# The inner groups of a three-stage layer kernel: a hardware loop or written out

## The reference

```python
x = x + xattn(layernorm(x), ctx, Wq, Wk, Wv, Wo, bo)   # 8 heads of 64, context 257 x 192 per sequence
x = x + attn(layernorm(x), ln_g, ln_b, Wx, Ww, bw, Wk, Wv, Wr, Wo)
#   w = sigmoid(xn @ Wx @ Ww + bw); k = xn @ Wk; v = xn @ Wv; r = sigmoid(xn @ Wr)
#   over the 32 rows: state = (1 - w) * state + k v^T;  out = r . state;  y = out @ Wo
x = x + ffn(layernorm(x), U1, V1, b1, U2, V2, b2)      # gelu(x @ U1 @ V1 + b1) @ U2 @ V2 + b2
```

## Time and profile before

| | |
|---|---|
| median of 3 runs | 1336.26 us (1333.10, 1336.26, 1339.06) |
| the profiled execution | 1338.63 us, span 1336.8 us |
| TensorE busy | 1109.4 us, 83% of the span |
| VectorE busy | 859.9 us, 64% |
| ScalarE busy | 788.3 us, 59% |
| GpSimd busy | 578.8 us, 43% |
| mean granted clock of TensorE | 0.973 |
| transfers | 73.88 MB, mean 55 GB/s |

### The profile page before, as it was taken

How to read it: one execution, slowest core, us unless ns; L and a number is a source line. 1 busy time by engine, 2 the same in 40 slices (tenths; PEclk the granted TensorE clock), 3 DMA queues, 4 the chain that set the end, 5 groups by cost and what they waited for, 6 DMA issues and landing times.

```text
span 1336.8 us, 26076 instructions
## 1 busy us (share of the span) xinstructions
PE 1109.4 (83%) x7880; PEld 906.3 (68%) x7880; DVE 859.9 (64%) x2340; ACT 788.3 (59%) x1886; POOL 578.8 (43%) x788
## 2 busy tenths in 40 slices
PE   3888888888888888888888888888888888888865
PEld 2767777685767758676676767667676776767643
DVE  3548477485856749477584857748485774848542
ACT  2656575665756556575665657566575756657521
POOL 1336245372534527254263625527362553725330
PEclk9899899999999999999999999999999999989976
DMA  6211112030221202122130211213021120302000
GB/s 231 75 47 57 50 51 71 22 99 14 63 64 43 75 22 69 44 63 58 33 91 22 63 50 55 64 35 91 22 63 50 49 69 22 102 11 63 21 8 8
DMA packets 49688, 73.88 MB, mean 55 GB/s; under 512 B 5697, under 2 KB 31425, under 8 KB 49665
## 3 DMA queue, kind: packets, MB, share of 16 engines
q1 hardware_dynamic: 42464, 65.06, 16.7%
q10 hardware_dynamic: 7200, 8.53, 1.9%
HBM read 68.98 MB, written 4.59 MB: 55 GB/s over the span
## 4 chain that ended last, share of the span: by engine, by line
PE 31%; issue 28%; DVE 23%; ACT 10%; POOL 6%; ACTq 1%; DVEq 1%; DMA 0%; POOLq 0%; SPq 0%
DVE probs L892 7%; PE gb L523 4%; PE gb L513 4%; PE gb L432 4%; ACT probs L690 3%; DVE xn L878 3%; PE scores L452 3%; PE gb L423 3%; PE ptp L470 2%; PE acc L491 2%; DVE ptl L905 2%; DVE tailp L900 2%; PE gb L415 2%; PE gb L579 2%; PE gb L588 1%
## 5 line engine op out<-in xcount | busy, mean ns | idle before, releaser
L1092 POOL TENSOR_TENSOR rstd<-ve,vecs 128x2 f32<-128x2 f32 x48 | 35.3, 736 | 395.8 <-DVE ve L869 395.8
L1075 POOL TENSOR_TENSOR t0l<-raw_t,t0h 128x258 fp32r<-128x258 f32 x128 | 95.2, 744 | 247.7 <-ACT t1s L679 247.7
L491 PE MATMUL acc<-pth,nat 128*128 128x256 f32 x768 | 172.8, 302 | 33.6 <-DVE ptl L905 33.2
L690 ACT ACTIVATE probs<-scores,nmax 128x257 f32<-128x257 f32 x256 | 119.1, 471 | 98.0 <-DVE nmax L885 97.8
L491 PEld LDWEIGHTS acc<-pth,nat 128*128 128x128 f32 x768 | 126.4, 188 | 48.4 <-DVE ptl L905 36.7
L470 PE MATMUL ptp<-ident_r,probs 128*128 128x128 f32 x512 | 84.3, 288 | 68.5 <-DVE probs L892 66.9
L491 PE MATMUL acc<-ptl,nat 128*128 128x256 f32 x512 | 137.4, 280 | 0.0
L979 DVE TENSOR_TENSOR qk_l<-gb,qk_h 128x512 fp32r<-128x512 f32 x128 | 83.8, 687 | 79.4 <-ACT qk_h L726 78.5
L702 ACT ACTIVATE pth<-ptp 128x512 fp32r<-128x512 f32 x128 | 76.6, 598 | 87.5 <-PE ptp L470 87.5
L706 ACT ACTIVATE pc<-acc 128x512 f32<-128x512 f32 x128 | 76.5, 598 | 81.2 <-PE acc L491 77.4
L892 DVE TENSOR_SCALAR probs<-probs,rinv 128x257 f32<-128x257 f32 x256 | 120.2, 511 | 4.5
(11 more groups left out here) (131 smaller groups left out, 3328.7 us busy)
## 6 DMA issues: line engine op xcount, KB each, us to landing
raw_t<-in_ctx_t SPq DMA_DIRECT2D x128, 258.0 KB, 2.8
raw_n<-in_ctx_n SPq DMA_DIRECT2D x128, 192.0 KB, 2.4
xin<-in_x SPq DMA_DIRECT2D x16, 256.0 KB, 2.9
out<-vt ACTq DMA_DIRECT2D x16, 256.0 KB, 3.5
tailc<-tail_scratch SPq DMA_DIRECT2D x64, 6.0 KB
wq<-in_wq SPq DMA_DIRECT2D x1, 512.0 KB, 3.7
wk_raw<-in_wk SPq DMA_DIRECT2D x1, 512.0 KB, 4.2
wo<-in_wo ACTq DMA_DIRECT2D x1, 512.0 KB, 5.2
```

What stands on the lines that cost most here:

```text
L491: last = mm(acc[:, i], w, x, start=k == 0, stop=k == len(terms) - 1)
L690: go(probs[:, r, 0:L], scores[:, r, 0:L], ACT.Exp, bias=nmax[:, r:r + 1], accum_out=rsum[:, r:r + 1]).then_inc(s["exp_ready"], 1)
L1075: p_.tensor_tensor(t0l[i][:], raw_t[i][:, 0], t0h[i][:].bitcast(F32), ALU.subtract)
```

## The change

`turns` calls the bodies for m = 0 to 13 with a number instead of opening a hardware loop, and so does SyncE. The order of instructions on each engine, their buffers and the values of all waits stay what they are; each wait is for a constant, each address is fixed. The program becomes longer: the loop's body stands in it fourteen times.

```diff
@@ turns @@
             body(Phase("a", 0))
             body(Phase("ab", 0))
-            with engine.Fori(0, NG - 2) as m:
+            for m in range(NG - 2):
                 body(Phase("abc", m))
             body(Phase("bc", 0))
             body(Phase("c", 0))
@@ block.sync, load_tails @@
-                    sp.dma_start(tailc[0:3, i:i + 2].bitcast(F32), scratch[:, bass.ds(g.index * G + 2 * pair, 2)])\
+                    sp.dma_start(tailc[0:3, i:i + 2].bitcast(F32), scratch[:, g.index * G + 2 * pair:g.index * G + 2 * pair + 2])\
                         .then_inc(tailc_in[pair % 2], 16)
@@ block.sync @@
             body(Phase("a", 0))
             body(Phase("ab", 0))
-            with sp.Fori(0, NG - 2) as m:
+            for m in range(NG - 2):
                 body(Phase("abc", m))
```

## The result

The changed kernel takes 1331.47 us (median of 16 runs, 1327.33 to 1333.82); the kernel before took 1334.55 beside it (16 runs, 1330.86 to 1339.06). The ratio is 0.9974, 95% interval 0.9962 to 0.9985: 3.1 us, a real gain, but a quarter of a per cent. Timed again later, the changed kernel gave 0.9969 (0.9958 to 0.9980). The result is inside the predicted range, on the forecast's side of no change, and less than half of the 8.4 us forecast; the prediction had called anything under 0.5% no more than "same".

What follows compares the result with a forecast made beforehand. No single engine bounded the kernel: TensorE held 31% of the chain of waits, VectorE 23%, "issue" 28%. Terms of 0.30 + 0.30 = 0.6 us a pass, times 14, took 8.4 from 1336.26, giving 1327.9 us; range 1315 to 1339.

Steps and rivals of the forecast that it cites:

- Registers, b = 2 to 7: Attention stretch between probability transposes of inner groups 2 and 7: register waits take 0.30 us a pass longer than constants.
- The twin: Written-out phase "ab", same work with constants: b = 2 to 7 takes 30.41 us against 30.71 in loop pass 2.
- hidden registers: Rival: the 0.30 us is another order of arrivals, handoffs are covered; time stays at 1336 (1331 to 1341); chance 0.20.
- more exposed: Rival: "issue" is partly registers in the uncompared 48 us; 1.3 us or more a pass, 1318 or less; chance 0.13.
- Handoffs elsewhere: Projections, b = 0 and 1, pass border: 0.14 us per handoff, two on the path, 0.30 us a pass (0 to 1.0).
- Branch and addresses: Engines' 14 jumps back and address arithmetic for 22 transfers a pass on SyncE and ScalarE: both worth 0.
- Code: Fetching written-out code all through the run costs 0.0 us; rival, packets waited for in full, 1374 us, chance 0.05.
- a gap that wanders: Sign of code cost: TensorE, VectorE or ScalarE gaps ending in "issue", moving through the pass with instruction packets.
- Clock: TensorE's clock falls at three of fifteen pass borders, one costing 2.84 us; a shorter period shifts them, direction unknown.
- the rival of 1362 us: TensorE's clock gives way at twelve more of fifteen pass borders, 2.84 us each, 34 us slower; clock rival's chance 0.10.
- The sum: Over 14 loop passes: 0.30 + 0.30 = 0.6 us a pass, 8.4 us less (ends 4 and 18), median 1327.9 us.

Runs made afterwards that it cites:

- late-wait kernel: Changed kernel with waits reordered so that the one ending last rides on the operation itself; 1330.97 us, ratio 0.9964 to the kernel before.

## Why the prediction was right, and where it was not

- **Registers, b = 2 to 7: the size right, the way only in part.** 0.30 forecast, 0.34 in this stretch, 0.29 over the pass; the kernel with VectorE alone written out has the 0.34. The prediction read the difference to "ab" as the price of register instructions in the path. At b = 3 to 4 these are at most 0.13 of the 0.55; 0.42 is the shorter pair at L892, and 0.3 is lost again behind it. The twin carried the same rearrangement, so the number came out; in that the rival "hidden registers", which spoke of another order of arrivals, was half right. Its forecast, a time unchanged, falls with the period, and so does "more exposed": the surplus of "issue" in the chain held no time that could be gained.
- **Handoffs elsewhere: the step that failed.** The term of 0.30 us a pass came from the one pair L979 and L432, which did gain (0.24 to 0.05). The step took it for the price of registers. It is the price of where the last wait stands, and writing out raises it at four other places by 0.10 each (L415 twice, L579, L985). The segment of a pass that holds the projections, between two of GpSimd's t0l steps, even takes 16.25 us instead of 16.06. The rest of the pass came out at 0.29 - 0.34 = -0.05, so the term was nothing, at its lower bound. That is also why the period, 78.29, reached neither the 77.9 to 78.1 that was to show the forecast right nor the 78.5 that was to show it wrong. 14 x 0.30 = 4.2 us of the 8.4 went there. Only a handoff that gains was read.
- **Branch and addresses: right**, worth 0; the period stayed at 78.55 with TensorE alone, and at 78.57 with ScalarE, GpSimd and SyncE.
- **Code: right.** 64 packets instead of 12 on the larger queue, four a pass where the prediction had three, and passes at full clock agree within 0.07 us, which leaves no room for a gap that wanders.
- **Clock: the open point was named, the form was not.** Falls did not spread to most borders, as the rival of 1362 us had it; the mean clock of the executions is that of before, 0.976. The changed kernel's falls cost 0.7 us each where before's cost 2.84. But the late-wait kernel shows the rival's mechanism at work: a pass 0.33 us shorter lost 0.54 us to falls, until the idle places were filled.
- **The sum.** 14 x 0.29 = 4.1 us by the period, 3.5 to 5.2 at an equal clock, 3.1 between the medians.

## What to carry to other kernels

Writing a loop out is worth what its registers cost on the engine that holds up the pass, here 0.29 us of 78.6, nearly all of it VectorE's. The "issue" share says nothing of it: look up in the timeline what the engine waited for there. Code the wait that ends last so that it rides on the operation, and look for 0.14 where 0.04 could be. And where a tuned kernel gets shorter and its time does not, read the clock by stretch and fill the engine's idle places before giving the change up.

## What the runs showed of the hardware

- One wait instruction between the last release and an operation costs 0.10 us: 0.04 when the wait rides on it, 0.14 with one instruction ahead; with registers, where two stand between (one of them register arithmetic that carries a wait), 0.23 to 0.24.
- A loop body of 68.5 KB on TensorE is held over its turns, with no instruction packet from 300 to 600 us; one of 137 KB is fetched anew, at 0.35 to 1.3 us a jump.
- The same two operations of VectorE (L892, b = 4) take 1.52 us or 1.10, after a shift of 0.2 us against GpSimd's work; that the overlap is the cause was not tested.
- Unused matmuls in idle places of 0.7 to 1.6 us, 32 a pass, raised the mean clock from 0.970 to 0.983 and took 12.5 us off (1330.97 to 1318.49).
